# A four-stage transformer block on one core: the order of GpSimd's key expansions, of one table load and of the first transposes in the second attention

## The chip, the cores and the metric

The kernel runs on one core of one Trainium2 chip. The metric is the device time of one execution in microseconds (us), the lower the better. Three runs of the kernel before gave 310.07 us as their median, the lowest 307.72 and the highest 310.26.

## The reference

The input x is 16 batches of 128 tokens with 128 features; a context holds 77 tokens for each batch. Four stages update x, each on the layer norm of x and each scaled by the tanh of a gate: an attention with one head, a mixture of 16 experts (4 of them for each token, and a shared one), a second attention with 16 heads of 8 features, and a mixture of 8 experts (2 for each token). The change lies in the second attention:

```python
q = query_states @ Wq.T + bq
k = key_value_states @ Wk.T + bk
v = key_value_states @ Wv.T + bv
q = q.reshape(B, SQ, NUM_HEADS, HEAD_DIM).transpose(0, 2, 1, 3) * SCALE
...
scores = jnp.einsum('bhqd,bhkd->bhqk', q, k)
attn = jax.nn.softmax(scores, axis=-1)
ctx = jnp.einsum('bhqk,bhkd->bhqd', attn, v)
ctx = ctx.transpose(0, 2, 1, 3).reshape(B, SQ, HIDDEN)
return ctx @ Wo.T + bo
```

## The kernel before

**Tiling.** Tokens lie on the 128 partitions. The 16 batches form four groups (g = 0 to 3) of four. The two mixtures and the norms go by group, 512 columns at a time; the two attentions go by batch inside a group. Each engine has its own program, written out by hand in the order in which it is to run, and semaphores tie the programs together. An engine's queue is strictly in order: an instruction that waits holds all that stand behind it on that engine. SyncE's queue only moves data; nothing of the second attention is loaded in that stage.

**The second attention, turn by turn.** Batch n = 4g + t is one turn, and the turns overlap. `kk` holds the keys of all batches with features on partitions. For a batch, GpSimd spreads its 77 keys into `KT` (`expand_keys`, L354): for each of the four heads that share a strip of 32 partitions, the keys times a mask, so that a matmul over the 32 rows gives four heads at once. `KT` has two slots, n mod 2. TensorE then makes the scores of the batch in four banks of PSUM (`c_scores`, L689, 16 products); it waits for the expanded keys (`ks_done`) and for VectorE to have read out the scores of the batch before (`c_sub`). VectorE takes the maximum and subtracts it, in two halves of eight heads (`c_max`, L1334, `c_center`, L1342). ScalarE takes the exponentials, also in two halves (`c_exps`, L966). TensorE transposes the probabilities in three parts (`c_transpose`, L699), the first from the first half alone and the others from both; ScalarE copies each part to SBUF (`c_copy`, L976). One turn later TensorE multiplies with the values (`c_mix`, L713), which GpSimd has placed in a block form (`place_values`, L418, five copies, two slots `VX`), and two turns later the result is normalised on VectorE (`c_normalize`, L1352 and L1355), transposed (`c_turn`, L722), copied by ScalarE, projected (`c_project`, L727) and added to x (`c_final`, L1364).

**TensorE's order in a turn** (`c_body`): scores of n + 1; first transpose of n; turn of n - 2; the other two transposes of n; projection of n - 2; first half of the mix of n - 1; once per group a transpose of the normed rows (`norm_T`, L482), the query of the next group or the router; second half of the mix of n - 1.

**GpSimd's order in a turn**: the expansion for n + 2 (waits for the scores of n), the placing for n + 1 (waits for the mix of n - 1); at t = 0 also the output bias added to the group's x (`add_bo`, L396); at t = 2 also the norm of the group after next: the inverse deviation from VectorE's variance (`inv_std`, L337), then two operations over 512 columns (`norm_apply`, L404 and L407). VectorE makes that variance in the same turn (`norm_stats`, L1045, L1049, L1052).

**The start of the stage.** TensorE makes the scores of batch 0 inside the last expert step of the first mixture (`c_begin`). ScalarE's last silu of the mixture is followed by the copy of the mixture's result (`m_y_copy`, L883, an Identity with a scale) and then by the exponentials of batch 0. TensorE turns that copy (`m_turn`, L580), VectorE adds it to x, and the first turn begins. Silu and exponential lie in different activation tables; the program that builds the kernel puts a table load in front of the first function that needs another table.

Of the kernel before, what the change touches and what calls it, by code (L numbers as in the profile page):

```python
# [8 lines left out]
ACT = mybir.ActivationFunctionType  # L9
AX = mybir.AxisListType.X  # L10

P = 128
NB = 16
S = 77
GB = 4
# [64 lines left out]
def flamingo(nc, x, ctxT, ctx, w0, w4, gate_router, w13, w2, up, down, consts, out, comb_rows):  # L80
    with ExitStack() as stack:
        at = [16512]

        def sb(name, shape, dt=F32, offset=None):

            size = 4
            for n in shape[1:]:
                size *= n
            if offset is None:
                offset = at[0]  # L90
                at[0] += -(-size // 32) * 32
            place[name] = offset
            return nc.alloc_sbuf_tensor_at(name, shape, dt, offset=offset)
# [35 lines left out]
        CB = sb("CB", [P, 4 * P + 28])  # L129
        I, B0 = CB[:, 0:P], CB[:, P:2 * P]  # L130
        bvc, tgbo = CB[:, 2 * P:3 * P], CB[:, 3 * P:4 * P]
        gbr, cols = CB[:, 4 * P:4 * P + 16], CB[:, 4 * P + 16:4 * P + 20]
        tg, mask4 = CB[:, 4 * P + 20:4 * P + 24], CB[:, 4 * P + 24:4 * P + 28]
        xn = sb("xn", [P, GT])
        W4 = sb("W4", [P, 4, P])
# [109 lines left out]
        def wait_apart(eng, semaphore, value):  # L245

            eng.wait_ge(semaphore, value)
            eng.sem_inc(passed[eng], 1)
# [76 lines left out]
        def _(pool):  # L325
# [22 lines left out]
            def expand_keys(n, par, first=False):  # L348

                if not first:  # L350
                    pool.wait_ge(c_sc, n - 1)
                keys = kk[:, :, bass.ds(n * S, S)].bitcast(F32).unsqueeze(2).to_broadcast([P, 2, HG, S])
                heads = mask4.unsqueeze(1).unsqueeze(3).to_broadcast([P, 2, HG, S])
                nc.gpsimd.tensor_tensor(KT[:, par].rearrange("p a (h k) -> p a h k", h=HG), keys, heads,  # L354
                                        ALU.mult).then_inc(ks_done, 1)
# [43 lines left out]
            def norm_apply(n, g):  # L399

                wait_apart(pool, xnT, n - 1)
                rows = [xn[:].rearrange("p (b d) -> p b d", b=GB),
                        X[:, bass.ds(g * GT, GT)].rearrange("p (b d) -> p b d", b=GB)]
                nc.gpsimd.tensor_tensor(rows[0], rows[1], mv[:, :, 0:1].to_broadcast([P, GB, P]),  # L404
                                        ALU.subtract).then_inc(centred, 1)
                wait_apart(pool, centred, n - 2 * NG - 1)
                nc.gpsimd.tensor_tensor(rows[0], rows[0], rstd[:].unsqueeze(2).to_broadcast([P, GB, P]),  # L407
                                        ALU.mult).then_inc(xn_rdy, 1)

            def place_values(n, par, first=False):  # L410

                if not first:
                    wait_apart(pool, c_pv, START + n - 1)
                src = VS[:, :, :, bass.ds(n, 1), :].rearrange("p (u j) i a d -> p u j i (a d)", u=NU)
                dst = VX[:, par].rearrange("p (u j) c -> p u j c", u=NU)
                for j in range(CU):
                    h, m = chunk_head(j), chunk_heads(j)
                    i = nc.gpsimd.tensor_copy(dst[:, :, j, h * HV:(h + m) * HV].rearrange("p u (i d) -> p u i d", i=m),  # L418
                                              src[:, :, j, 0:m])
                i.then_inc(vx_rdy, 1)  # L420

            def c_body(g, last):
                for t in range(GB):
                    if not (last and t >= GB - 2):
                        expand_keys(GB * g + t + 2, t % 2)
                    if not (last and t == GB - 1):
                        place_values(GB * g + t + 1, (t + 1) % 2)
                    if t == 0:
                        add_bo(g)
                    if t == 2 and not last:  # L430
                        inv_std(2 * NG + 3 + g)
                        norm_apply(2 * NG + 3 + g, (g + 2) % NG)
# [12 lines left out]
            pool.wait_ge(bo_rdy, 1)  # L445
            inv_std(2 * NG + 2)
            norm_apply(2 * NG + 2, 1)
            with pool.Fori(0, NG - 1) as g:
                c_body(g, False)
            c_body(NG - 1, True)  # L450
# [5 lines left out]
        def _(pe):  # L456
# [236 lines left out]
            def c_transpose(g, t, r):  # L693
                n = GB * g + t
                pe.wait_ge(c_exp, NU * n + (1 if r == 0 else 2))
                pe.wait_ge(c_ev, START + 3 * n + (1 if r == 2 else 0))
                for c in range(4 * r, min(NC, 4 * r + 4)):
                    w = chunk_rows(c)
                    i = tr(bP[r][0:w, c % 4 * P:c % 4 * P + P], PX[:, t % 2, chunk_col(c):chunk_col(c) + w], I)  # L699
                i.then_inc(c_tr, 1)  # L700
# [28 lines left out]
            def c_body(g, last):  # L729

                for t in range(GB):
                    n = GB * g + t
                    if n + 1 < NB:
                        c_scores(*divmod(n + 1, GB))
                    c_transpose(g, t, 0)
                    if t == 1:
                        pe.wait_ge(xl_rdy, NG + g + 2)
                    if t == 2 and not last:
                        pe.wait_ge(q_l, g + 2)
                    if t == 2 and last:  # L740
                        pe.wait_ge(route["vals"], mD.route_base + 1)
                    if n >= 2:
                        c_turn(*divmod(n - 2, GB))
                    c_transpose(g, t, 1)
                    c_transpose(g, t, 2)
                    if n >= 2:
                        c_project(*divmod(n - 2, GB))
                    if n:
                        c_mix(*divmod(n - 1, GB), n == 1, 0)
                    if n >= 2 and (t < 2 or last and t == GB - 1):  # L750
                        pe.wait_ge(c_fin, START + n - 1)
                    if t == 0:
                        pe.wait_ge(x_done, START + 2 * NG)
                        norm_T(2 * NG + 2 + g)
                    if t == 1 and last:
                        m_logits(mD, 0)
                    if t == 1 and not last:
                        c_query(g + 1)
                    if t == GB - 1 and last:
                        m_route_T(mD, 0)  # L760
                    if n:
                        c_mix(*divmod(n - 1, GB), n == 1, 1)
# [43 lines left out]
        def _(act):  # L806
            A = nc.scalar.activation
# [71 lines left out]
            def m_y_copy(m, g):  # L879

                act.wait_ge(m.dn, START + m.units * (g + 1))
                act.wait_ge(m.y_tr, START + g)
                A(ysb[:], Ybank[:, bass.ds(slot(g), GT)], ACT.Identity, scale=tg[:, m.tg:m.tg + 1]).then_inc(m.y_cp, 1)  # L883

            def m_body(m, g, nxt, then=None, begun=0):

                for k in range(m.units):
                    if k >= begun:
                        m_silu(m, g, k)
                    if then:  # L890
                        then(k)
                    if k == 1 and used(g, 0):
                        m_y_copy(m, g - 1)
                    if k == 2 and m.shared:
                        act.wait_ge(sh_up, g + 1)
                        if used(g, 0):
                            act.wait_ge(sh_lo, g)
                        A(hs[:], Eb[64:P, :], ACT.Silu).then_inc(sh_silu, 1)
                    if k == 3 and m.shared:
                        act.wait_ge(sh_hid, g + 1)  # L900
                        if used(g, 0):
                            act.wait_ge(m.dn, START + m.units * (g - 1) + 5)
                        A(hst[0:64, :], hs[:], ACT.Copy).then_inc(sh_hi, 1)
                    if nxt is not None and k == 2:
                        norm_hi(nxt[0], xh[:, bass.ds(slot(nxt[2]), GT)])
                    if nxt is not None and nxt[1] is not None and k == 3:
                        m_route_act(nxt[1], nxt[2])
                    if nxt is not None and nxt[1] is not None and k == m.units - 3:
                        m_route_tanh(nxt[1], nxt[2])
                    if nxt is not None and nxt[1] is not None and k == m.units - 2:  # L910
                        m_route_copy(nxt[1], nxt[2])
# [97 lines left out]
                    c_query(0)  # L1009

            m_body(m, NG - 1, (2 * NG + 1, None, 0), c_ahead)
            m_y_copy(m, NG - 1)
            for u in range(NU):
                c_exps(0, 0, u)
# [463 lines left out]
```

## Time and profile before

| what | value |
|---|---|
| median of three runs (lowest, highest) | 310.07 us (307.72, 310.26) |
| the profiled execution, its own time | 309.45 us |
| span of the profiled execution | 307.6 us |
| granted TensorE clock, mean over the span | 0.988 |
| busy: TensorE, its weight loads, VectorE, ScalarE, GpSimd | 278.5, 209.3, 235.0, 130.8, 87.6 us |
| second attention, first scores to the second mixture's first product | 130.2 to 220.4 us |

The span runs from the first to the last instruction; 1.85 us of the execution's own time lie around it. The busy times come from the page's first part. The stage's borders are the first L689 and the first product with the second mixture's weights on the timeline. In the rows, PE is TensorE, PEld its weight loads, DVE VectorE, ACT ScalarE, POOL GpSimd; "idle before" in square brackets is the time that the engine had nothing running, with the work that ended it.

### The profile page before, as it was taken

The page shows a single profiled execution, that of the slowest core. Times are in us where ns is not written, and L with a number is a line of the kernel's source. Part 1 is how long each engine was busy: PE and PEld are TensorE (multiplying, and loading weights), DVE is VectorE, ACT ScalarE, POOL GpSimd, SP SyncE. Part 2 cuts the span into 40 slices and gives each one's busy share as a digit, 9 for nine tenths or more (in the row PEclk, how much of TensorE's full clock was granted, in tenths as well). Part 3 has the DMA queues.
Part 4 walks back from the last instruction along what each step waited for, and adds up shares of the span by engine and source line. Part 5 has one row for each costly group of instructions (what it writes and reads, how often), then busy time and mean ns, then how long its engine had stood idle before and what let it go on. Part 6 is the DMA issues. An engine that isn't in the chain of part 4 may idle for free.

```text
span 307.6 us, 5453 instructions
## 1 busy us (share of the span) xinstructions
PE 278.5 (91%) x1646; PEld 209.3 (68%) x1646; DVE 235.0 (76%) x660; ACT 130.8 (43%) x275; POOL 87.6 (28%) x162
## 2 busy tenths in 40 slices
PE   6799869988999979969989899899899999999994
PEld 5589547666656646637878788789767676676661
DVE  2887879947888998787977977887568869777572
ACT  1497623242234323276656556464622332422330
POOL 8376130100082041452555654751110100100000
PEclk9999979997999999999999999999999999999999
DMA  6900056163143243000000000000043051430640
GB/s 216 351 39 1 4 199 183 52 211 114 41 140 131 48 148 120 26 0 2 2 1 2 0 2 3 0 2 1 6 155 116 29 210 39 153 107 19 233 145 34
DMA packets 15066, 25.26 MB, mean 82 GB/s; under 512 B 2341, under 2 KB 4339, under 8 KB 14835
## 3 DMA queue, kind: packets, MB, share of 16 engines
q1 hardware_dynamic: 12968, 23.88, 23.8%
q10 hardware_dynamic: 2072, 1.07, 1.3%
q8 instruction: 13, 0.21, 0.3%
q14 instruction: 13, 0.11, 0.1%
HBM read 22.98 MB, written 1.25 MB: 79 GB/s over the span
## 4 chain that ended last, share of the span: by engine, by line
PE 67%; DVE 9%; DMA 8%; ACT 5%; issue 4%; POOL 4%; SPq 2%; POOLq 0%; DVEq 0%; ACTq 0%
PE S L542 24%; PE Ybank L564 15%; PE Ybank L713 9%; DMA CR<-comb_rows 4%; PE bank L699 4%; PE S L689 3%; ACT pt L976 2%; DMA comb_rows<-ct 2%; PE Tb L482 2%; DMA X<-in_x 2%; DVE cmx L1334 1%; SPq L307 1%; PE bank L580 1%; POOL KT L354 1%; DVE xn L1059 1%
## 5 line engine op out<-in xcount | busy, mean ns | idle before, releaser
L861 ACT ACTIVATE sg<-S 128x512 f32<-128x512 f32 x64 | 38.1, 597 | 75.4 <-PE S L542 67.2
L1205 DVE TENSOR_TENSOR hb<-sg,CR 128x512 f32<-128x512 f32 x64 | 44.6, 697 | 15.0 <-issue 5.9
L1198 DVE TENSOR_TENSOR sg<-sg,S 128x512 f32<-128x512 f32 x64 | 43.5, 680 | 3.4 <-PE S L542 2.1
L337 POOL TENSOR_TENSOR rstd<-ve,mhalf 128x4 f32<-128x4 f32 x11 | 11.1, 1011 | 111.5 <-DVE ve L1052 111.5
L713 PE MATMUL Ybank<-VX,pt 128*128 128x128 f32 (+1 forms) x320 | 39.7, 275 | 0.0
L542 PE MATMUL S<-xh,WBH 128*128 128x512 f32 x64 | 34.6, 540 | 5.1 <-DVE kk L1125 2.7
L713 PEld LDWEIGHTS Ybank<-VX,pt 128*128 128x128 f32 (+1 forms) x320 | 37.9, 192 | 0.4
L542 PE MATMUL S<-xh,UPH 128*128 128x512 f32 x64 | 36.1, 564 | 0.0
L564 PE MATMUL Ybank<-hb,downw 128*128 128x512 f32 x64 | 33.0, 599 | 0.4 <-DVE hb L1205 0.4
L564 PE MATMUL Ybank<-hb,W2T 128*128 128x512 f32 x64 | 33.1, 602 | 0.0
L1334 DVE TENSOR_REDUCE cmx<-S 128x8 f32<-128x616 f32 x32 | 25.4, 794 | 4.6 <-PE S L689 4.3
L418 POOL COPY VX<-VS 128x36 f32 (+3 forms) x80 | 13.7, 220 | 47.5 <-PE Ybank L713 39.7
L1342 DVE TENSOR_TENSOR PX<-S,cmx 128x616 f32<-128x616 f32 x32 | 25.6, 799 | 1.1
L966 ACT ACTIVATE PX<-PX 128x616 f32<-128x616 f32 x32 | 22.7, 712 | 8.7 <-DVE PX L1342 8.7
L542 PE MATMUL S<-xl,WBH 128*128 128x512 f32 x64 | 26.0, 405 | 0.0
L542 PE MATMUL S<-xh,WBL 128*128 128x512 f32 x64 | 25.9, 405 | 0.0
L542 PE MATMUL S<-xh,UPL 128*128 128x512 f32 x64 | 25.2, 394 | 0.0
L542 PE MATMUL S<-xl,UPH 128*128 128x512 f32 x64 | 25.0, 391 | 0.0
L976 ACT ACTIVATE pt<-bank 128x512 f32<-128x512 f32 (+1 forms) x32 | 15.7, 490 | 18.1 <-PE bank L699 17.9
L542 PEld LDWEIGHTS S<-xh,WBH 128*128 128x128 f32 x64 | 12.6, 196 | 15.0 <-DVE sg L1198 6.7
L354 POOL TENSOR_TENSOR KT<-kk,CB 128x616 fp32r<-128x616 f32 x16 | 19.7, 1234 | 5.8 <-PE S L689 5.8
L699 PE MATMUL bank<-CB,PX 128*128 128x128 f32 x96 | 16.9, 285 | 3.0 <-ACT pt L976 3.0
(164 smaller groups left out, 502.9 us busy)
## 6 DMA issues: line engine op xcount, KB each, us to landing
CR<-comb_rows SPq DMA_DIRECT2D x64, 128.0 KB, 3.1
CR<-comb_rows SPq DMA_DIRECT2D x32, 256.0 KB, 3.3
w13raw<-in_w SPq DMA_DIRECT2D x1, 1088.0 KB, 11.0
X<-in_x SPq DMA_DIRECT2D x4, 256.0 KB, 6.2
upraw<-in_up SPq DMA_DIRECT2D x4, 256.0 KB, 4.0
out_x<-X SPq DMA_DIRECT2D x4, 256.0 KB, 3.3
cT<-in_ctxT SPq DMA_DIRECT2D x2, 308.0 KB, 5.6
CN<-in_ctx SPq DMA_DIRECT2D x1, 616.0 KB
```

Source lines behind the costliest of these rows:

```text
L354: nc.gpsimd.tensor_tensor(KT[:, par].rearrange("p a (h k) -> p a h k", h=HG), keys, heads, ALU.mult).then_inc(ks_done, 1)
L542: i = mm(dst, wp[:, col:col + P], xp[:, bass.ds(xs, GT)], start=n == 0, stop=n == 2)
L564: mm(Ybank[:, bass.ds(slot(g), GT)], m.wd[:, k, :], hb[:, k % 2, :], start=k == 0, stop=k == m.units - 1, skip_group_check=True).then_inc( ...
L699: i = tr(bP[r][0:w, c % 4 * P:c % 4 * P + P], PX[:, t % 2, chunk_col(c):chunk_col(c) + w], I)
L713: i = mm(bO9[u], pt[0:w, t % 2, c * P:(c + 1) * P], VX[0:w, t % 2, c, :], start=c % CU == 0, stop=c % CU == CU - 1)
L861: A(sg[:, k % 2, :], Gb[k % 2][:], ACT.Silu).then_inc(m.s_done, 1)
L966: A(p, p, ACT.Exp).then_inc(c_exp, 1)
L976: A(pt[:, t % 2, 4 * r * P:4 * r * P + w], bPa[r][:, 0:w], ACT.Copy).then_inc(c_ev, 1)
L1198: V.tensor_tensor(sg[:, k % 2, :], sg[:, k % 2, :], Ub[k % 2][:], ALU.mult).then_inc(m.t2, 1)
L1205: V.tensor_tensor(hb[:, k % 2, :], sg[:, k % 2, :], CR[:, k % RING, :], ALU.mult).then_inc(m.h_done, 1)
L1334: V.tensor_reduce(cmx[:, 2 * u:2 * u + 2, :], pair(u), AX, ALU.max, negate=True).then_inc(c_mx, 1)
L1342: V.tensor_tensor(PX[:, t % 2, u * UK:(u + 1) * UK].rearrange("p (s h k) -> p s h k", s=2, h=HG), pair(u), cmx[:, 2 * u:2 * u + 2, :].unsq ...
```

## The change

Three things are changed, all of them an order of work. First, GpSimd runs its expansions one turn further ahead in the text: before the loop it expands the keys of batch 2, and in turn n it first places the values of n + 1 and then expands the keys of n + 3, both ahead of the bias (t = 0) and of the norm (t = 2). Second, ScalarE gets one more instruction: an exponential over one column of the constants (`spare`, a column of zeros that nothing else reads), behind the last silu of the first mixture and ahead of the copy of its result. Third, in turn 0 alone TensorE has the first transpose of batch 0 ahead of the scores of batch 1 instead of behind them. No wait is added or taken away, and no transfer is touched.

```diff
--- before.py
+++ after.py
@@ -130,6 +130,7 @@
         I, B0 = CB[:, 0:P], CB[:, P:2 * P]
         bvc, tgbo = CB[:, 2 * P:3 * P], CB[:, 3 * P:4 * P]
         gbr, cols = CB[:, 4 * P:4 * P + 16], CB[:, 4 * P + 16:4 * P + 20]
+        spare = CB[:, 4 * P + 19:4 * P + 20]
         tg, mask4 = CB[:, 4 * P + 20:4 * P + 24], CB[:, 4 * P + 24:4 * P + 28]
         xn = sb("xn", [P, GT])
         W4 = sb("W4", [P, 4, P])
@@ -421,10 +422,10 @@
 
             def c_body(g, last):
                 for t in range(GB):
-                    if not (last and t >= GB - 2):
-                        expand_keys(GB * g + t + 2, t % 2)
                     if not (last and t == GB - 1):
                         place_values(GB * g + t + 1, (t + 1) % 2)
+                    if not (last and t >= GB - 3):
+                        expand_keys(GB * g + t + 3, (t + 1) % 2)
                     if t == 0:
                         add_bo(g)
                     if t == 2 and not last:
@@ -445,6 +446,7 @@
             pool.wait_ge(bo_rdy, 1)
             inv_std(2 * NG + 2)
             norm_apply(2 * NG + 2, 1)
+            expand_keys(2, 0)
             with pool.Fori(0, NG - 1) as g:
                 c_body(g, False)
             c_body(NG - 1, True)
@@ -730,9 +732,12 @@
 
                 for t in range(GB):
                     n = GB * g + t
+                    if n == 0:
+                        c_transpose(g, t, 0)
                     if n + 1 < NB:
                         c_scores(*divmod(n + 1, GB))
-                    c_transpose(g, t, 0)
+                    if n:
+                        c_transpose(g, t, 0)
                     if t == 1:
                         pe.wait_ge(xl_rdy, NG + g + 2)
                     if t == 2 and not last:
@@ -1009,6 +1014,7 @@
                     c_query(0)
 
             m_body(m, NG - 1, (2 * NG + 1, None, 0), c_ahead)
+            A(spare, spare, ACT.Exp)
             m_y_copy(m, NG - 1)
             for u in range(NU):
                 c_exps(0, 0, u)
```

## Rows read from the trace of the kernel before

**Rows 1.** The page's first part: busy time, share of the span, instructions.

```profile
PE 278.5 (91%) x1646; PEld 209.3 (68%) x1646; DVE 235.0 (76%) x660; ACT 130.8 (43%) x275; POOL 87.6 (28%) x162
```

**Rows 2.** The page's fourth part: the chain that ended last, by engine.

```profile
PE 67%; DVE 9%; DMA 8%; ACT 5%; issue 4%; POOL 4%; SPq 2%; POOLq 0%; DVEq 0%; ACTq 0%
```

**Rows 3.** Windows: width, busy PE, PEld, DVE, ACT, POOL, then PEclk, DMA, GB/s.

```profile
154.38:176.38 22.00, 20.30 (x204) 18.02 (x203) 18.01 (x39) 12.81 (x27) 12.39 (x29) 1.00 0.00 1
176.38:198.38 22.00, 20.30 (x204) 18.03 (x203) 18.02 (x39) 12.81 (x27) 12.38 (x29) 1.00 0.01 2
```

**Rows 4.** Waits of TensorE, 130 to 221 us: us in total, times, longest.

```profile
PE S L689 <- DVE PX L1342: 2.0, 2, 1.2
PE S L689 <- POOL KT L354: 1.8, 3, 0.6
```

**Rows 5.** The chain, 148 to 156 us: start, length, what.

```profile
153.81 1.18 POOL KT L354
```

**Rows 6.** The timeline, 148 to 162 us: start, length, what, [idle].

```profile
149.18 0.84 PE L689 MATMUL S<-KT,qq 32*128 32x308 f32 x16
149.50 0.86 POOL L418 COPY VX<-VS 128x36 f32 x5 [2.97 <-PE Ybank L713]
...
150.30 0.17 DVE L1052 TENSOR_SCALAR ve<-mv 128x4 f32<-128x4 f32 x1
...
151.01 0.33 PE L722 MATMUL Tb<-CB,On 128*128 128x128 f32 x1 [0.40 <-DVE On L1355]
...
152.05 2.40 PE L713 MATMUL Ybank<-VX,pt 128*128 128x128 f32 x20
...
153.44 0.80 DVE L1342 TENSOR_TENSOR PX<-S,cmx 128x616 f32<-128x616 f32 x1
153.77 1.21 POOL L354 TENSOR_TENSOR KT<-kk,CB 128x616 fp32r<-128x616 f32 x1
...
154.93 0.86 POOL L418 COPY VX<-VS 128x36 f32 x5
...
155.04 0.84 PE L689 MATMUL S<-KT,qq 32*128 32x308 f32 x16 [0.59 <-POOL KT L354]
...
158.83 0.60 PE L482 MATMUL Tb<-CB,xn 128*128 128x128 f32 x4
...
161.61 1.27 POOL L396 TENSOR_TENSOR X<-X,CB 128x512 f32 x1
```

**Rows 7.** The timeline, 168 to 170 us.

```profile
169.12 0.29 DVE L1364 TENSOR_TENSOR X<-Tb,X 128x128 f32<-128x128 f32 x1 [0.43 <-PE Tb L727]
```

**Rows 8.** The timeline, 128 to 140 us: the start of the second attention.

```profile
131.96 0.80 DVE L1342 TENSOR_TENSOR PX<-S,cmx 128x616 f32<-128x616 f32 x1
132.17 0.69 ACT L883 ACTIVATE ysb<-Ybank,CB 128x512 f32<-128x512 f32 x1 [3.63 <-PE Ybank L564]
...
132.88 1.28 ACT L966 ACT_TABLE_LOAD   x1
...
133.50 0.80 DVE L1342 TENSOR_TENSOR PX<-S,cmx 128x616 f32<-128x616 f32 x1
134.17 1.33 ACT L966 ACTIVATE PX<-PX 128x616 f32<-128x616 f32 x2
...
134.44 0.84 PE L689 MATMUL S<-KT,qq 32*128 32x308 f32 x16 [0.88 <-DVE PX L1342]
...
138.65 0.84 PE L689 MATMUL S<-KT,qq 32*128 32x308 f32 x16 [1.15 <-DVE PX L1342]
```

**Rows 9.** The timeline, 108.9 to 109.3 us: VectorE beside an expansion of keys.

```profile
108.94 1.44 POOL L354 TENSOR_TENSOR KT<-kk,CB 128x616 fp32r<-128x616 f32 x1
...
109.22 1.25 DVE L1059 TENSOR_SCALAR xn<-X,mv,rstd 128x128 f32 x1
```

**Rows 10.** Instructions of line 1059: nanoseconds min/median/max.

```profile
L1059 DVE TENSOR_SCALAR xn<-X,mv,rstd x28: 328/343/1956, 38.4 to 264.5; 128x128 f32<-128x128 f32 x20, 128x128 f32 x8
```

**Rows 11.** Instructions of line 1052, the variance plus epsilon.

```profile
L1052 DVE TENSOR_SCALAR ve<-mv x11: 169/171/171, 36.8 to 262.4; 128x4 f32<-128x4 f32 x11
```

## The prediction, made before the changed kernel had run

> **What bounds the kernel now.** I read the page's first part, then the chain that ended last, then the second attention alone by windows, by TensorE's waits and on the timeline. The first part shows TensorE busy for 91% of the span [rows 1], and the chain gives it 67%, GpSimd 4% [rows 2]: time is won where TensorE stands idle, and only if what it waits for can come sooner. The windows from the scores of batch 5 to those of batch 9, and on to batch 13, have the same 22.00 us each, with 20.30 us of TensorE in them; VectorE, the next, has 18.0 [rows 3]. So each group loses 1.7 us of TensorE. The waits say where the scores have a share in it: three waits for GpSimd's expanded keys, 1.8 us in all, and two for VectorE's centring, 2.0 us, at the start of the stage [rows 4].
>
> The timeline shows how the wait for keys arises. In turn 2 of group 0 GpSimd places the values at 149.50 and is free at 150.36; then comes the norm for a later group (inverse deviation and two wide operations), and the keys of batch 5 follow only at 153.77. They are the chain's own piece there [rows 5]. TensorE ends its mix at 152.05 + 2.40 = 154.45 and begins the scores of batch 5 at 155.04, idle for 0.59 [rows 6]. The norm's result, ahead of which nobody was waiting, is not turned before 158.83 [rows 6]. The pattern repeats every 22.00 us, three times in all by the count of [rows 4]; the last group makes no norm in its turn 2.
>
> **Part 1, GpSimd's order.** The text moves by one turn, but the order of expansions and placings among themselves stays what it was (keys 2, values 1, keys 3, values 2, keys 4, ...). What really changes is that the keys of 4g + 3 go ahead of the bias and those of 4g + 5 ahead of the norm; 16 expansions and 16 placings remain, no transfer is issued by GpSimd, and no queue is passed. The keys of batch 5 need the scores of batch 3, over long before 149.18. So they run from about 150.3 to 151.6 (1.21 us, the length of the row at 153.77) and are 2.8 us ahead of the 154.4 at which TensorE can use them.
>
> What is late next: the scores also wait for VectorE's centring, which ends at 153.44 + 0.80 = 154.24, and for TensorE's own mix. From the end of a centring to the scores is 0.14 us (133.50 + 0.80 = 134.30, then 134.44 [rows 8]), so 154.38; and the scores at 149.18 show how closely they can follow a mix that ends at about the same time. I take 154.38 to 154.45 as the new start, a gain of 155.04 - 154.4 = 0.65 us, and of 0.59 by TensorE's idle time alone. Three times: 1.8 to 2.0 us, 1.95 taken, the start by the centring being the one the other turns show. It is kept, since in that group everything behind it follows from TensorE's scores.
>
> What waits behind the moved expansion: the norm ends 1.21 us later, at about 155.0 instead of 153.8; it is turned at 158.83 less the 0.65, so 3 us of cover. The values at 154.93 wait for the mix in any case; GpSimd finishes the same work by then, so they stay. The bias starts 1.2 us later, at about 162.8, and ends by 164.1; its reader, the first addition of the group's turn, is at 169.12 [rows 7]. All three are costed at nothing; if a cover were gone, each would cost at most its 1.21 us per group.
>
> **Part 2, the table load.** ScalarE is idle for 3.63 us before the copy at 132.17. The load (1.28 us) and a tiny exponential fit into that from 128.54 on, with over 2 us left. The first exponential can then start behind the copy, at 132.86 + 0.02, instead of 134.17: its centring was over at 131.96 + 0.80 = 132.76. At 0.67 us each (1.33 for the two) it ends at 133.6 instead of 134.8. The second half still waits for its centring, over at 134.30, and ends at 135.0 instead of 135.5 [rows 8].
>
> **Part 3, the first transpose ahead of the scores.** With the exponential there at 133.6, four transposes (0.60 us, as four take at 158.83 [rows 6]) run between 133.65 and 134.3, in TensorE's idle time of 0.88 us before the scores at 134.44. The scores of batch 1 do not move, since they wait for the centring that ends at 134.30. Then VectorE has the stage's start in hand: maximum and centring twice, and the scores of batch 2 wait for that at 138.65, with TensorE idle for 1.15 us [rows 8]. The transposes taken out of the stretch between 134.44 and 138.65 only make this idle time longer. Parts 2 and 3 together: 0. Bounds: if the order held the scores of batch 1 back until an exponential at the old time, 134.17 + 0.67, and the issue of four transposes, they would start 0.9 us late; if all of the idle 0.88 could be used, 0.9 us would be won. I stay at 0 between them, because the row at 138.65 names the centring as its releaser.
>
> **Sum.** The profiled execution: 309.45 - 1.95 = 307.5 us. The median of the three runs is 0.6 above that execution: 310.07 - 1.95 = 308.1 us.
>
> **A rule against the change.** The rows show that VectorE and GpSimd can block each other. A normalising operation of line 1059 that takes 0.343 us as a rule took 1.25 when it began at 109.22 beside an expansion that had begun at 108.94 and ended at 110.38 [rows 9, 10]. In the changed order an expansion begins when the placing of 149.50 is over, at 150.36 or a few hundredths before, and VectorE's variance operation of line 1052 runs from 150.30 to 150.47 [rows 6]: a tie within the reading. It takes 0.17 us in all its 11 executions [rows 11], also where it began in the last hundredths of a placing, but never beside a beginning expansion. The Trainium skill (SBUF — State Buffer, section Who interferes with whom) says that a VectorE operation in a mode that uses both ports and a GpSimd operation share a pair of ports as an exclusive lock: whichever issues first holds it to its end. The trace agrees as far as 1.25 against 0.343 goes. By that rule alone the sum would hang on a tie, and this is the first rival.
>
> **The rivals.** (a) *Slower: the expansion takes the port ahead of the variance operation.* Then that operation ends at about 151.6 instead of 150.47, and everything behind it in VectorE's queue is about 1.15 us later: the normalisation for which TensorE already waits 0.40 at 151.01, and the centring that ended at 154.24, now 155.4. The scores of batch 5 start at 155.4 + 0.14 = 155.53 instead of 155.04: 0.5 us lost in place of 0.65 won, three times +1.5, so 311.6 us by the median (310.9 against the profiled execution). It decides as soon as the port is held for more than 0.65 us. For it: the tie, and the rows of line 1059. Against it: VectorE's operation asks for 4 elements and is first by the reading, and the row at 149.50 did not lengthen it. (b) *Nothing is won*: another wait, VectorE's centring or the mix, stands where the keys stood, or the keys do not come earlier because a wait ahead of them on GpSimd's queue does the same. The centring's 154.24 speaks against it. 310.1 us. (c) *More is won*: 3 x 0.65 at the keys and the 0.88 at the start, 310.07 - 2.8 = 307.2 us; for it speaks only that this idle time is there. (d) *The start loses 0.9 us* because the load isn't where it should be or the exponential is late, with part 1 as forecast: 309.0 us. That the change does not do what it says would show here: the load could stay in front of the first real exponential.
>
> **How the numbers follow.** Forecast 0.58, (a) 0.14, (b) 0.10, (c) 0.08, (d) 0.10. The predicted time is 308.1 us. The three runs before lie up to 2.35 us below and 0.2 above their own median, so a median of few runs can fall lower than the cases say: low is 308.1 - 2.3 = 305.8, which takes in (c). High is 311.2: above (b) and (d) with that spread, and into (a), of which a part stays outside. A measurement of this kernel can tell about 1% from no change, 3.1 us. Faster by more than that asks for less than 307.0: (c) with a little, or the forecast with low runs, 0.13. Slower by more asks for over 313.2: only (a) with more than its price, 0.03. Within 1%: 0.84.
>
> **What would show each step.** Right, if in the profile after (part 1) the waits of the scores for keys are gone, the window of a group is about 21.35 us instead of 22.00, and the norm's second operation ends near 155 with its turn not waiting; (part 2) a table load starts at about 128.6 and none stands between the copy and the exponential; (part 3) the first transposes run before the scores of batch 1, which still start at about 134.4 and batch 2's at 138.65. Wrong, if line 1052 has executions of over 1 us and TensorE's wait at L722 has grown to 1.6 us (rival a); if the scores of 4g + 5 still wait, now for L1342 or for nothing shown (b); if batch 2's scores start a good deal before 138.65 (c), or batch 1's at 135.3 (d).

## The result, and the profile after

The changed kernel took 310.00 us as the median of 14 runs (306.87 to 313.42), the kernel before 307.49 us of 14 (305.13 to 310.75): a ratio of 1.0064, 95% interval 1.0032 to 1.0095. The ratios here and below leave out executions in a slower state, four of the changed kernel's 14, which the medians contain; five of the profiles below are of such an execution, and their stages agree with those of the others. Measured once more the ratio was 1.0040, with an interval (0.9996 to 1.0085) that just reaches no change. It was forecast 1.95 us faster and came out about 2 us slower, 1.2 us by the second measurement.

The profiled execution of the changed kernel shows 308.63 us, less than the 309.45 of the one before, and is of no use as a total: the first mixture, where nothing was changed, ended 3.4 us earlier in it (first scores at 126.88 instead of 130.24). In the profile before, the granted clock was below 1.00 from 40 to 48 us and from 70 to 80 us (0.64 from 40 to 44, 0.69 from 70 to 75); in the profile after, it is 1.00 in all of the first mixture. The stage has to be measured by itself, from the first scores to the second mixture's first product. It was 90.15 us before and is 92.54 after. The 2.39 us lie in two places. The line numbers of the changed kernel are a little higher: L724 is the old L722, L1058 the old L1052, L1348 the old L1342.

**First place: turns 2 and 3 of each group.** The timeline after, group 0 (start, length, what, idle before), answers to [rows 6]:

```profile
146.92 0.84 PE L691 MATMUL S<-KT,qq 32*128 32x308 f32 x16
147.24 0.86 POOL L419 COPY VX<-VS 128x36 f32 x5 [2.97 <-PE Ybank L715]
...
148.05 1.25 DVE L1058 TENSOR_SCALAR ve<-mv 128x4 f32<-128x4 f32 x1
148.06 1.22 POOL L355 TENSOR_TENSOR KT<-kk,CB 128x616 fp32r<-128x616 f32 x1
...
149.21 0.24 DVE L1358 RECIPROCAL rec<-Ybank 128x16 f32<-128x16 f32 x1
...
149.49 0.29 DVE L1361 TENSOR_TENSOR On<-Ybank,rec 128x128 f32<-128x128 f32 x1
...
149.84 0.33 PE L724 MATMUL Tb<-CB,On 128*128 128x128 f32 x1 [1.49 <-DVE On L1361]
...
152.26 0.80 DVE L1348 TENSOR_TENSOR PX<-S,cmx 128x616 f32<-128x616 f32 x1
...
153.21 0.84 PE L691 MATMUL S<-KT,qq 32*128 32x308 f32 x16
```

The keys of batch 5 are there at 149.3, as forecast, and the scores at 153.21 wait for no keys. But VectorE's variance operation, started at 148.05 beside the expansion of 148.06, takes 1.25 us and ends when the expansion does. Behind it in VectorE's queue stand the reciprocal and the normalisation, for which TensorE waits 1.49 us at L724 (0.40 in [rows 6]), and the centring, which ends at 153.06. All instructions of that operation, against [rows 11] (nanoseconds min/median/max):

```profile
L1058 DVE TENSOR_SCALAR ve<-mv x11: 170/170/1261, 37.2 to 261.4; 128x4 f32<-128x4 f32 x11
```

TensorE's waits in the stage (total, times, longest), against [rows 4]; the wait for keys is gone, and the first line is the new one:

```profile
PE Tb L724 <- DVE On L1361: 5.7, 4, 1.5
PE S L691 <- DVE PX L1348: 2.3, 2, 2.1
PE bank L701 <- ACT pt L981: 2.3, 10, 0.2
```

**Second place: the start.** The timeline after, against [rows 8]:

```profile
125.20 1.28 ACT L1017 ACT_TABLE_LOAD   x1
...
128.82 0.69 ACT L888 ACTIVATE ysb<-Ybank,CB 128x512 f32<-128x512 f32 x1 [2.12 <-PE Ybank L566]
...
129.44 0.72 ACT L971 ACTIVATE PX<-PX 128x616 f32<-128x616 f32 x1
...
130.26 0.63 PE L701 MATMUL bank<-CB,PX 128*128 128x128 f32 x4
...
131.10 0.84 PE L691 MATMUL S<-KT,qq 32*128 32x308 f32 x16 [0.21 <-DVE PX L1348]
...
132.58 0.60 PE L484 MATMUL Tb<-CB,xn 128*128 128x128 f32 x4
...
135.31 1.22 PE L691 MATMUL S<-KT,qq 32*128 32x308 f32 x16 [2.13 <-DVE PX L1348]
```

The load stands at 125.20, far ahead of the copy; the exponential starts at 129.44, when its centring is over; the transposes (L701) run in the idle time before the scores of batch 1, and those start 4.22 us behind the scores of batch 0 (4.20 before). All of that was forecast. The last row was not: the scores of batch 2 take 1.22 us instead of 0.84, because the granted clock falls about 0.25 us after they begin (it is 0.74 in their first 0.5 us and 0.50 behind that). Windows of both kernels from the scores of batch 1 to those of batch 2, and on to batch 3 (width, busy PE, PEld, DVE, ACT, POOL, then PEclk, DMA, GB/s), before:

```profile
134.44:138.65 4.21, 2.71 (x31) 2.11 (x32) 3.60 (x6) 3.70 (x8) 1.31 (x2) 1.00 0.00 0
138.65:144.18 5.53, 5.19 (x51) 4.50 (x51) 4.04 (x6) 3.69 (x7) 0.00 (x0) 1.00 0.01 3
```

and after, with one group (batch 5 to 9) behind them, against [rows 3]:

```profile
131.10:135.31 4.21, 2.08 (x27) 1.66 (x28) 3.70 (x6) 3.28 (x7) 2.45 (x2) 1.00 0.00 0
135.31:141.91 6.60, 6.60 (x49) 5.73 (x49) 3.83 (x6) 3.77 (x7) 0.00 (x0) 0.74 0.01 2
153.21:175.64 22.43, 20.24 (x205) 18.03 (x204) 19.12 (x39) 12.81 (x27) 12.46 (x28) 1.00 0.00 1
```

TensorE is idle for 2.13 us before the scores of batch 2 instead of 1.15. The granted clock is 0.74 in the mean of the 6.60 us that follow, that is, 1.2 GHz in about the first half of them and 2.4 GHz in the rest, and TensorE is busy through all of that window: 1.07 us more than the 5.53 at the full clock. The groups are 22.43 us instead of 22.00.

### The profile page after: what moved, and what is told of

Its sections match the earlier page's. It is cut to its first block, busy times and chain, and to the rows that moved or that the text cites. A ratio compares the mean times of both kernels' runs of the same rounds, so it can differ in the third digit from the quotient of the medians.

```text
span 306.8 us, 5457 instructions
## 1 busy us (share of the span) xinstructions
PE 276.4 (90%) x1646; PEld 207.9 (68%) x1646; DVE 238.7 (78%) x660; ACT 130.9 (43%) x276; POOL 88.0 (29%) x162
## 3 DMA queue, kind: packets, MB, share of 16 engines
q10 hardware_dynamic: 2072, 1.07, 1.3%
HBM read 22.98 MB, written 1.25 MB: 79 GB/s over the span
## 4 chain that ended last, share of the span: by engine, by line
PE 71%; DVE 13%; DMA 7%; issue 4%; ACT 4%; SPq 1%; DVEq 0%
PE S L544 25%; PE Ybank L566 16%; PE Ybank L715 9%; PE bank L701 4%; PE S L691 3%; DMA CR<-comb_rows 3%; DVE cmx L1340 2%; ACT pt L981 2%; PE Tb L484 2%; DMA X<-in_x 2%; DVE xn L1065 2%; DVE PX L1348 2%; DMA comb_rows<-ct 1%; PE Tb L729 1%; PE bank L582 1%
## 5 line engine op out<-in xcount | busy, mean ns | idle before, releaser
L544 PE MATMUL S<-xh,WBH 128*128 128x512 f32 x64 | 33.2, 518 | 5.8 <-DVE sg L1204 3.0
L1348 DVE TENSOR_TENSOR PX<-S,cmx 128x616 f32<-128x616 f32 x32 | 25.6, 800 | 1.1
L544 PE MATMUL S<-xh,WBL 128*128 128x512 f32 x64 | 25.2, 394 | 0.0
L544 PE MATMUL S<-xl,WBH 128*128 128x512 f32 x64 | 25.1, 392 | 0.0
L701 PE MATMUL bank<-CB,PX 128*128 128x128 f32 x96 | 17.6, 294 | 2.4 <-ACT pt L981 2.3
```

The source lines that it names most:

```text
L544: i = mm(dst, wp[:, col:col + P], xp[:, bass.ds(xs, GT)], start=n == 0, stop=n == 2)
L1348: V.tensor_tensor(PX[:, t % 2, u * UK:(u + 1) * UK].rearrange("p (s h k) -> p s h k", s=2, h=HG), pair(u), cmx[:, 2 * u:2 * u + 2, :].unsq ...
```

## The experiments

Lengths of the stage in the profiled execution of each kernel, in us: from the scores of batch 0 to batch 1, to 2, to 3, to 4, and from there to the end of the stage. "Idle" is TensorE's idle time before the scores of batch 2. The ratio is that of the times to the kernel before, with its 95% interval.

| kernel | 0-1 | 1-2 | 2-3 | 3-4 | rest | stage | idle | ratio (interval) |
|---|---|---|---|---|---|---|---|---|
| before | 4.20 | 4.21 | 5.53 | 5.00 | 71.21 | 90.15 | 1.15 | 1 |
| changed | 4.22 | 4.21 | 6.60 | 5.01 | 72.50 | 92.54 | 2.13 | 1.0064 (1.0032-1.0095) |
| changed, again | 4.22 | 4.21 | 6.59 | 5.01 | 72.49 | 92.52 | 2.13 | 1.0040 (0.9996-1.0085) |
| part 1 alone | 4.22 | 4.21 | 6.71 | 5.00 | 72.51 | 92.65 | 1.17 | 1.0021 (0.9981-1.0061) |
| parts 2 and 3 | 4.22 | 4.20 | 6.62 | 5.00 | 71.24 | 91.28 | 2.12 | 0.9984 (0.9951-1.0018) |
| part 2 alone | 4.21 | 4.20 | 5.52 | 5.00 | 71.21 | 90.14 | 1.15 | 1.0028 (0.9994-1.0063) |
| part 3 alone | 5.30 | 4.21 | 6.63 | 5.01 | 71.23 | 92.38 | 2.15 | 1.0056 (1.0020-1.0091) |
| part 1 behind the variance | 4.22 | 4.20 | 5.52 | 5.00 | 69.24 | 88.18 | 1.16 | 0.9930 (0.9892-0.9968) |
| all, behind the variance | 4.20 | 4.21 | 6.60 | 5.00 | 69.25 | 89.26 | 2.13 | 0.9871 (0.9824-0.9919) |
| the same, again | 4.21 | 4.20 | 6.66 | 5.00 | 69.23 | 89.30 | 2.12 | 0.9962 (0.9927-0.9998) |
| all, variance by a reduction | 4.21 | 4.20 | 6.76 | 5.01 | 69.23 | 89.41 | 2.12 | 0.9968 (0.9927-1.0009) |
| parts 2 and 3, five products | 4.21 | 4.20 | 5.70 | 5.00 | 71.22 | 90.33 | 0.96 | 0.9989 (0.9958-1.0019) |
| all, behind the variance, five products | 4.21 | 4.20 | 5.69 | 5.00 | 69.25 | 88.35 | 0.96 | 0.9948 (0.9916-0.9979) |
| part 1 behind the variance, four products | 4.22 | 5.08 | 5.54 | 5.00 | 69.24 | 89.08 | - | 0.9942 (0.9907-0.9977) |

**Part 1 alone.** Only the two edits on GpSimd of the diff.

> The first part alone: GpSimd's order is that of the changed kernel, ScalarE's and TensorE's are those of the kernel before. Theory (the shared port): each of the three variance operations (L1052) that meets a beginning expansion takes about 1.25 us instead of 0.17, TensorE's wait at L722 in those turns is about 1.5 us, and the second attention from its first scores to the second mixture's first product is about 90.15 + 1.3 = 91.45 us long; the time is about 1.3 us above the kernel before (ratio 1.004). Rival (the loss is all from the start of the stage, and the expansions cost or give what was forecast): 1.9 us below the kernel before (ratio 0.994), the stage 88.2 us.

Its operation has the changed kernel's long executions, and the rest of the stage is 1.30 us longer than before, the changed kernel's 1.29:

```profile
L1053 DVE TENSOR_SCALAR ve<-mv x11: 169/170/1258, 36.8 to 263.6; 128x4 f32<-128x4 f32 x11
```

The rival is out. The stage was 92.65 us and not 91.45, since the clock fell here too, after only 1.17 us of idle time and about 0.8 us behind the start of the scores of batch 2 (which still took 0.84 us). The ratio, 1.0021, leaves the rival's 0.994 out but does not resolve 1.3 us.

**Parts 2 and 3 without part 1.** The edits on ScalarE and TensorE of the diff.

> The second and third part alone: the exponential table loaded behind the last silu and the first transpose of batch 0 ahead of the scores of batch 1, with GpSimd's old order. Theory (the clock): TensorE stands idle for about 2.1 us before the scores of batch 2, its granted clock falls to 1.2 GHz there, those scores take about 1.2 us instead of 0.84 and the stage is about 1.1 us longer, 91.2 us; ratio 1.0035. The first scores of batch 1 are not later than before. Rival (the order alone costs nothing, and the low clock seen in the changed kernel was chance): the stage 90.15 us, ratio 1.000, clock 1.00 from the scores of batch 2 on.

```profile
135.19:139.39 4.20, 2.08 (x27) 1.66 (x27) 3.70 (x6) 3.28 (x7) 1.31 (x2) 1.00 0.01 4
139.39:146.01 6.62, 6.62 (x50) 5.75 (x50) 3.84 (x6) 3.79 (x7) 0.00 (x0) 0.74 0.00 0
```

The windows from the scores of batch 1 and of batch 2 show the low clock (0.74) as in the changed kernel, and the stage is 91.28 us. The clock fell 0.5 us after the scores began, so these took 1.01 us and not 1.2. By the trace the theory holds; by the times it does not: 0.9984, and its interval leaves 1.0035 out. More on that below.

**Part 1 with the expansion behind the variance.**

```diff
+                    if t == 2 and not last:
+                        pool.wait_ge(var_rdy, 2 * NG + 3 + g)
                     if not (last and t >= GB - 3):
                         expand_keys(GB * g + t + 3, (t + 1) % 2)
```

> The first part with one wait more: in turn 2 of a group GpSimd waits for VectorE's variance (var_rdy, for which it waits a moment later in any case) before it expands the keys of 4g + 5, so that the expansion can't begin beside the variance operation. Theory (the shared port): L1052 takes 0.17 us everywhere, no wait of the scores for keys, the group 21.35 us, the stage 90.15 - 1.9 = 88.2 us, ratio 0.994. Rival (the longer variance operation is a symptom and not the cause: VectorE is behind anyway once the keys come early): the stage stays at 90.2 or above, ratio 1.000 or more.

```profile
149.43 0.17 DVE L1055 TENSOR_SCALAR ve<-mv 128x4 f32<-128x4 f32 x1
...
149.79 1.22 POOL L354 TENSOR_TENSOR KT<-kk,CB 128x616 fp32r<-128x616 f32 x1 [0.30 <-DVE ve L1055]
149.79 0.29 DVE L1358 TENSOR_TENSOR On<-Ybank,rec 128x128 f32<-128x128 f32 x1
...
152.56 0.80 DVE L1345 TENSOR_TENSOR PX<-S,cmx 128x616 f32<-128x616 f32 x1
...
153.51 0.84 PE L692 MATMUL S<-KT,qq 32*128 32x308 f32 x16
```

The variance takes 0.17 us, the expansion begins 0.19 us after its end (149.60, 149.79), and the scores of batch 5 follow the centring (152.56 + 0.80) after 0.15 us. The normalisation that starts with the expansion at 149.79 takes its usual 0.29 us. A group is 21.34 us long in the mean (22.00 - 1.97 / 3), where 21.35 was forecast. The stage is 88.18 us, where 88.2 was expected; the ratio 0.9930 stands beside 0.994. So the cost of part 1 is the meeting of these two instructions and nothing else, and the 1.95 us of the prediction were there to be had (71.21 - 69.24 = 1.97).

**All three parts behind the variance**, with the same two lines, twice.

> All three parts with the same wait for the variance ahead of the expansion. Theory (the two costs are separate and add up): the stage 90.15 - 1.9 + 1.1 = 89.3 us, ratio 0.997, with the low clock at the scores of batch 2. Rival (the low clock has to do with the expansions): as the kernel with the first part and the wait alone, 88.2 us, ratio 0.994.

The stage is 89.26 us: the two costs are separate and add up. The first ratio, of 6 runs, was far below the traces, so it was repeated on one chip with the changed kernel:

> The changed kernel once more, on the same chip as the three beside it, since the kernel with the wait for the variance differed from it by more (0.987 against 1.006, on two chips) than the traces give. Theory (port lock three times, 1.3 us, and a clock drop at the scores of batch 2): ratio to the kernel before 1.004 to 1.007, no execution with a mean granted clock above 0.995. Rival (the first measurement was high by chance or chip): ratio 1.000 or less.

> All three parts with the wait for the variance ahead of the expansion, once more (only 6 runs the first time). Theory: the stage 89.3 us against 92.5 of the changed kernel, so 3.2 us (0.0105 in the ratio) below the changed kernel on the same chip. Rival (the wait does more than keep the port free): 4 us or more below it in the mean of executions with equal clock.

The changed kernel came out at 1.0040, with no execution above 0.994 in mean clock. The medians on this chip are 308.94 and 306.12 us, 2.8 apart, against 3.2 by the stages (92.52 and 89.30). Among executions of equal clock (0.993 and 0.994, both measurements of both kernels) the means are about 308.1 and 304.1 us. That is the 4 us that the rival named, though from 12 and 10 executions only; the traces show no more than 3.2, and where the rest would lie was not found.

**The variance by another operation.** This kernel leaves out the epsilon.

```diff
-                V.tensor_scalar(ve[:], mv[:, :, 1], EPS, None, ALU.add).then_inc(var_rdy, 1)
+                V.tensor_reduce(ve[:], mv[:, :, 1:2], AX, ALU.max).then_inc(var_rdy, 1)
```

> The changed kernel with another operation in the place of L1058: the variance is taken over by a reduction over one element, without the epsilon of 1e-5 (left out in the norms made by that helper, all but those of the first attention). It reads and writes the same SBUF tiles at the same moment, beside the same beginning expansion. Theory (the lock is taken only by forms of operation that use the second port, as tensor_scalar between SBUF tiles does and a reduction does not): the operation takes about 0.17 us everywhere and the stage is 89.3 us, as with the wait for the variance; ratio 0.996. Rival (any VectorE operation on SBUF waits for an expansion that has begun): 1.25 us three times, the stage 92.5 us, ratio 1.004.

```profile
L1058 DVE TENSOR_REDUCE ve<-mv x11: 157/157/160, 37.6 to 258.1; 128x4 f32<-128x4 f32 x11
```

Its place in group 0:

```profile
148.04 0.16 DVE L1058 TENSOR_REDUCE ve<-mv 128x4 f32<-128x4 f32 x1
148.05 1.22 POOL L355 TENSOR_TENSOR KT<-kk,CB 128x616 fp32r<-128x616 f32 x1
```

It starts 0.01 us ahead of the expansion, as in the changed kernel, and never takes over 0.16 us. The rest of the stage is 69.23 us, as with the wait. So it is not the meeting of the engines that costs, but the form of VectorE's operation. The Trainium skill (SBUF — State Buffer, section Who interferes with whom) names `tensor_scalar` among the forms that can take the shared ports and says of `tensor_reduce` that it never contends on trn2. The runs agree with both, 1.25 us against 0.16.

**The start with five products more.** Five products that nobody reads fill part of TensorE's idle time.

```diff
                         norm_T(2 * NG + 2 + g)
+                    if n == 0:
+                        for _ in range(5):
+                            mm(Ybank[:, GT:2 * GT], WQH[:], xh[:, 0:GT], start=True, stop=True)
```

> The second and third part alone, with five products of 512 columns more in turn 0 on TensorE, behind the transpose of the normed rows, into a part of PSUM that is free then; their result is read by nobody. They lie in the idle time before the scores of batch 2. Theory (TensorE's idle time there makes the granted clock fall): the idle time is about 0.9 us instead of 2.13, the clock stays at 2.4 GHz, those scores take 0.84 us and the stage is 90.15 us as in the kernel before; some executions have a mean clock of 0.998 or more, of which the same kernel without the five had none in 13. Rival (the clock falls for another reason at this place): the drop stays, 91.2 us.

```profile
136.41 1.41 PE L761 MATMUL Ybank<-xh,WQH 128*128 128x512 f32 x5
138.77 0.84 PE L690 MATMUL S<-KT,qq 32*128 32x308 f32 x16 [0.96 <-DVE PX L1350]
```

> All three parts, the wait for the variance, and the five products. Theory: the stage 90.15 - 1.9 = 88.2 us, 1.1 us below the same without the products, ratio about 0.993 or less. Rival (the drop moves to another place or stays): no difference to the kernel without the products, 89.3 us.

In both kernels the idle time is 0.96 us, the scores take 0.84, and the clock is 1.00 in the window behind them. That window is 5.70 and 5.69 us instead of 6.6; 0.16 to 0.17 of the loss is left. So the low clock follows from TensorE's idle time there and not from the order of the transposes. The products make the idle time shorter and the work in that turn longer at once (TensorE busy for 3.24 us of 4.20 instead of 2.08 of 4.21); no run separates these two. The mean granted clock of every execution says how general that is. A drop as in the changed kernel's profile takes (1 - 0.74) x 6.60 = 1.7 us of full clock out of some 307, or 0.006 of the mean, so an execution that has it can't be much above 0.994. Seven measurements are of kernels with 2.1 us of idle time, 81 executions: none is above 0.994. The others, with the kernel before, are 171 executions, and 38 of them are at 0.996 or more. Among the kernels with about 1.15 us of idle time the drop was in one profile of four (part 1 alone, where 4 of the 12 executions are at 0.996 or more and so were without it). In the times the five products show nothing clear: 0.9989 against 0.9984, measured on two chips, and 0.9948 against 0.9962 on one, that is 0.4 us where the stages differ by 0.95 and 1.1 was expected.

**Part 2 alone and part 3 alone.**

> The second part alone: the exponential table loaded behind the last silu. TensorE's order is the old one, but the exponentials are there sooner, so the transposes behind the scores of batch 1 end sooner and the idle time before the scores of batch 2 grows from 1.15 us to about 1.6. Theory of the clock: the longer the idle time, the surer the drop; stage 90.15 us without it and 91.2 with it, no more than chance for either. Rival (the drop hangs on the order, not on the idle time): never a drop, 90.15 us. Neither expects a gain: the scores of batch 1 and 2 stay where VectorE's centring puts them, 4.2 and 8.4 us behind those of batch 0.

> The third part alone: the first transpose of batch 0 ahead of the scores of batch 1, the table loaded in front of the first real exponential as before. Theory: the transposes wait for an exponential that ends at 3.9 us + 0.67 behind the scores of batch 0, and the scores of batch 1 start about 5.0 us behind them instead of 4.2: 0.8 to 0.9 us lost, stage 91.0 us (92.1 with a clock drop), ratio 1.003 to 1.006. Rival (the order does not matter): 90.15 us, ratio 1.000.

Part 2 alone changes nothing: the idle time stayed at 1.15 us, not 1.6, since the first transposes stand behind the scores of batch 1 in any case and the copies behind them wait for the transposes. Its profile has no drop, so it does not tell its theory from its rival. Part 3 alone (the load, the transposes, the scores of batch 1 and 2):

```profile
134.71 1.28 ACT L969 ACT_TABLE_LOAD   x1
...
136.82 0.63 PE L699 MATMUL bank<-CB,PX 128*128 128x128 f32 x4 [1.42 <-issue]
...
137.38 0.84 PE L689 MATMUL S<-KT,qq 32*128 32x308 f32 x16
...
141.59 0.71 PE L689 MATMUL S<-KT,qq 32*128 32x308 f32 x12 [2.15 <-DVE PX L1345]
```

The transposes hold the scores of batch 1 back by 1.1 us (5.30 instead of 4.20), more than the 0.8 to 0.9 expected, and the drop comes on top. So part 2 is what keeps part 3 from costing this, and both together win nothing.

**The old start with four products.**

> The first part with the wait for the variance, the old order at the start of the stage, and four products of 512 columns more in turn 0, read by nobody, in TensorE's idle time before the scores of batch 2 (1.15 us, so some of them may push those scores by 0.1 us or so). Theory: the stage 88.2 to 88.4 us in every execution, ratio 0.993 or less, the best so far. Rival (in the old order the clock hardly ever drops there, and the products cost only): no better than without them, ratio 0.993 to 0.995.

```profile
134.25:139.33 5.08, 5.08 (x36) 4.10 (x36) 3.72 (x6) 3.91 (x8) 2.46 (x2) 0.66 0.02 3
```

Neither in the trace: in its profile the clock fell one turn earlier, ahead of the products, behind the idle 0.88 us before the scores of batch 1 (the same 0.88 us stands in four other profiles without a drop). At the low clock TensorE was busy through the whole turn and the products were themselves in the way (5.08 instead of 4.21). The stage was 89.08 us, so "in every execution" was wrong; the ratio 0.9942 is in the rival's range.

The best stage is that of part 1 behind the variance, 88.18 us, with nothing changed at the start. Its ratio 0.9930 (0.9892 to 0.9968) is below both kernels; the two with products more (0.9942, 0.9948) and all three parts behind the variance (0.9871 and 0.9962) can't be told from it by the times.

## Why the prediction was wrong

**Part 1, the keys.** The idle time, its release and its size were right: free of the port, the change gives 1.97 us where 1.95 was taken. The step that failed is the weighing of the rule against the change: the 0.65 us a group stood on a variance operation that still takes 0.17 us beside the moved expansion, and it took 1.25 to 1.26 us in all three groups, so that a group became 22.43 us long and not 21.35. The prediction saw the tie (an expansion at about 150.3, the variance at 150.30), priced the case where the expansion takes the port at +0.5 us a group, and gave it 0.14, because the operation asks for 4 elements, is first by the reading, and was not lengthened where it began in the last hundredths of a placing. None of the three kept the case away. The size did not matter, the placing of [rows 6] says nothing of an expansion, and after the change the operation is still first by the reading, by 0.01 to 0.02 us, and was held in all groups. What it measured is 1.29 us over three groups (71.21 to 72.50) beside the rival's +1.5, with TensorE's wait of 1.49 at L724 beside its 1.6. Rival (a) is what happened.

**Parts 2 and 3, the start.** Right: the load hidden, the exponential at the end of its centring, the transposes in the idle time, the scores of batch 1 and 2 where they were. Wrong: "the transposes taken out of the stretch ... only make this idle time longer", costed at 0. It is the idle time of the engine that had all the following turn to carry, and behind 2.13 us of it (1.15 before) the granted clock fell, which cost 1.07 us by the trace. None of the rivals had this.

**The sum.** By the stage, 1.29 + 1.07 = 2.36 of the 2.39 us measured. By the times, 307.49 x 0.0064 = 2.0 us, interval 1.0 to 2.9. The port's 1.3 us is shown: the rest of the stage is 72.49 to 72.51 us in the three profiles with the long operation, 71.21 to 71.24 in the five with the old order on GpSimd, 69.23 to 69.25 in the six with the new order and a short operation. Of the clock's 1.07 it is shown that it stands in every profile with 2.1 us of idle time (7 of 7) and goes with that time (and with the work that fills it). How much of it the medians carry is open: parts 2 and 3 alone had the drop and were not slower than the kernel before, which has drops of its own in the first mixture (from 40 to 48 and 70 to 75 us in its profile, mean clocks 0.64, 0.93 and 0.69 in those windows).

**The base.** The 310.07 us of three runs was high by itself: 14 runs gave 307.49. The forecast ratio, 1 - 1.95 / 310.07 = 0.994, lies in the interval of part 1 behind the variance (0.9930). That the 310.00 us fell inside the stated 305.8 to 311.2 was luck: the base stood 2.6 us too high and the range was widened for its spread, while the time itself moved the other way.

## What to carry to other kernels

When a long GpSimd operation is moved, look at every VectorE instruction that it will now lie beside, however small, and at its form: one `tensor_scalar` over 4 elements between SBUF tiles, started as the expansion started, held VectorE's whole queue for 1.25 us; a `tensor_reduce` in its place did not. A tie in the trace of before is no reason for a low chance; one more wait on GpSimd, or another form on VectorE, takes the case away. And work taken out of a stretch in which TensorE waits is not free: count how long the engine then stands idle, since what follows may run at half its clock.

## What was not expected of the hardware

- Of two instructions on VectorE and GpSimd that start within 0.01 to 0.02 us of each other in the trace, VectorE's first (148.05 and 148.06), GpSimd's kept its 1.22 us and VectorE's, a `tensor_scalar` over 4 elements, was held to its end; the same in all groups and in two more profiles (part 1 alone, the changed kernel again), with 1.25 to 1.26 us.
- The granted clock fell to 1.2 GHz behind 2.12 to 2.15 us of idle time in 7 of 7 profiles, behind 1.15 to 1.17 us in 1 of 4, and behind 0.96 us in none of 2; and once in the turn before, where the idle time was 0.88 us (1 of 5 profiles with that idle time). It fell not at the end of the idle time but 0.1 to 1.5 us after TensorE had begun the next scores (by windows of 0.5 us), so in two of the seven profiles those scores still took 0.84 us and the work behind them was slow.
